# A state-space stage with the jobs of five engines in another order over its 32 scan steps

## The reference

```python
x = x + mamba(layernorm(x), ...)       # the stage that is changed
x = x + moe_ffn(layernorm(x), ...)     # 8 experts, top 2, capacity 80
x = x + attention(layernorm(x), ...)
x = x + moe_ffn(layernorm(x), ...)

# mamba, d_inner = 512, d_state = 16
xc, z = split(x @ in_proj_w + in_proj_b)
xc = silu(depthwise_conv(xc, 4 taps) + conv_b)
delta_s, B, u = split(xc @ x_proj_w + x_proj_b)
delta = softplus(delta_s @ dt_proj_w + dt_proj_b)
h[t] = exp(-n * delta[t]) * h[t-1] + delta[t] * B[t] * u[t]   # n = 1..16
y[t] = sum over the 16 states of h[t]
out = ((y + u * D) * silu(z)) @ out_proj_w + out_proj_b
```

## Time and profile before

| | us |
|---|---|
| three runs | 3225.42, 3229.64, 3231.66 (median 3229.64) |
| the profiled execution | 3236.31, span 3234.5 |
| first and last scan start | 75.9 and 1659.7 |
| busy over the span: PE, PE weight loads | 2880.0, 2285.2 |
| busy over the span: DVE, ACT, POOL | 2343.9, 1760.0, 2186.3 |
| POOL's products dbu, 512 of them | 1198.1 |
| DVE's scans, 512 of them | 1145.4 |
| ACT's decays da, 1024 of them | 571.3 |

### The profile page before, as it was taken

How to read it: one execution, slowest core, us unless ns; L and a number is a source line. 1 busy time by engine, 2 the same in 40 slices (tenths; PEclk the granted TensorE clock), 3 DMA queues, 4 the chain that set the end, 5 groups by cost and what they waited for, 6 DMA issues and landing times. The chain is left out here.

```text
span 3234.5 us, 54379 instructions
## 1 busy us (share of the span) xinstructions
PE 2880.0 (89%) x16992; PEld 2285.2 (71%) x16992; DVE 2343.9 (72%) x4219; ACT 1760.0 (54%) x3332; POOL 2186.3 (68%) x1405
## 2 busy tenths in 40 slices
PE   5899989999899898999857999996999985999998
PEld 2566666666666665666547999996777775999998
DVE  2998889888898888988965666564566654666564
ACT  3766767667676566766534444452333333444443
POOL 2888988889888898899955555552233435565554
PEclk8999999999999999999978999997999997999999
DMA  4231222112221122211244445442222223444443
GB/s 106 104 112 67 81 74 71 45 55 81 75 73 42 55 81 76 72 44 53 74 159 137 115 105 129 94 116 53 76 85 85 89 80 111 116 111 110 105 116 48
DMA packets 192660, 281.60 MB, mean 87 GB/s; under 512 B 35943, under 2 KB 164622, under 8 KB 184264
## 3 DMA queue, kind: packets, MB, share of 16 engines
q1 hardware_dynamic: 157128, 236.31, 22.1%
q0 software_dynamic: 35328, 42.76, 7.4%
HBM read 197.28 MB, written 94.72 MB: 90 GB/s over the span
## 5 line engine op out<-in xcount | busy, mean ns | idle before, releaser
L605 POOL TENSOR_TENSOR dbu<-du,bb 128x1024 f32<-128x1024 f32 x512 | 1198.1, 2362 | 66.2 <-DVE hs L755 63.0
L755 DVE TENSOR_TENSOR_SCAN hs<-da,dbu 128x1024 f32<-128x1024 f32 x512 | 1145.4, 2275 | 49.4 <-POOL dbu L605 20.9
L690 ACT ACTIVATE da<-delta 128x512 f32<-128x512 f32 x1024 | 571.3, 595 | 270.2 <-DVE hs L755 249.4
L855 PEld LDWEIGHTS yT<-ident,hs 128*128 128x128 f32 x4096 | 501.7, 150 | 162.3 <-issue 115.1
L855 PE MATMUL yT<-ident,hs 128*128 128x128 f32 x4096 | 552.2, 288 | 27.4 <-DVE hs L755 27.2
L1322 POOL TENSOR_TENSOR ffn_w_lo<-ffn_w,ffn_w_hi 128x512 fp32r<-128x512 f32 x256 | 344.1, 1370 | 177.8 <-ACT ffn_w_hi L1317 173.6
L1368 PE MATMUL ffn_hbank<-ffn_rowsT_hi,ffn_w_hi 128*128 128x320 f32 x1024 | 341.4, 333 | 43.7 <-DVE ffn_hT_lo L1390 41.5
L1402 PE MATMUL ffn_ybank<-ffn_w_hi,ffn_hT_hi 128*128 128x256 f32 x1280 | 365.1, 285 | 0.7 <-DVE ffn_hT_lo L1390 0.7
L1404 PE MATMUL ffn_ybank<-ffn_w_hi,ffn_hT_lo 128*128 128x256 f32 x1280 | 359.5, 281 | 0.0
L1403 PE MATMUL ffn_ybank<-ffn_w_lo,ffn_hT_hi 128*128 128x256 f32 x1280 | 359.3, 281 | 0.0
L1370 PE MATMUL ffn_hbank<-ffn_rowsT_hi,ffn_w_lo 128*128 128x320 f32 x1024 | 322.2, 315 | 0.0
(11 more groups left out here) (237 smaller groups left out, 5271.1 us busy)
## 6 DMA issues: line engine op xcount, KB each, us to landing
bb<-b_rows SPq DMA_DIRECT2D x64, 1024.0 KB, 4.5
ffn_w<-L_ffn_W SPq DMA_DIRECT2D x64, 1024.0 KB, 10.1
slots<-empty SPq DMA_DIRECT2D x40, 530.0 KB, 6.5
ffn_rows<-slots SPq DMA_DIRECT2D x32, 662.5 KB, 5.0
a_x<-x_after_mamba SPq DMA_DIRECT2D x32, 512.0 KB
xt<-L_attn_a_x SPq DMA_DIRECT2D x16, 512.0 KB
x<-L_attn_a_x SPq DMA_DIRECT2D x16, 512.0 KB, 4.1
x_after_mamba<-x SPq DMA_DIRECT2D x16, 512.0 KB, 2.9
```

The source lines that it names most:

```text
L605: pool.tensor_tensor(dbu[:, s % DEEP], du[:, dt, :].unsqueeze(1).to_broadcast([P, SN, T]), bb[:, q * SN:(q + 1) * SN, :], ALU.mult).then_i ...
L690: ins = act.activation(da[:, s % 2, i, :], delta[:, par, dt, :], ACT.Exp, scale=-float(q * SN + i + 1))
L755: dve.tensor_tensor_scan(flat[0], flat[1], flat[2], 0.0, ALU.mult, ALU.add).then_inc(scanned.sem, 1)
L855: mm = pe.matmul(yT[:, j * P:(j + 1) * P], hs[:, s % DEEP, i, j * P:(j + 1) * P], k.ident[:], start=False, stop=(q == QS - 1 and i == SN - ...
```

## The change

The arithmetic and the number of instructions stay. What changes is at which of the 32 steps each engine does its other jobs, the order of jobs within some steps, and with that the four lists of orders, and so the bank of some jobs in the ring and the job whose reader they wait for: O0 goes ahead of T0 and T1, I1 ahead of O1, and RP ahead of Z3. No step's own work (dbu, da, scan, sum) moves.

```diff
-RING_JOBS = ("G3", "Z0", "U2", "T0", "O0", "T1", "U3", "I0", "O1", "I1", "G0", "Z1", "I2", "I3", "S", "RT0", "RT1",
-             "DA0", "DA1", "DA2", "DA3", "G1", "RL", "U0", "Z2", "U1", "G2", "Z3", "RP", "-")
+RING_JOBS = ("G3", "Z0", "U2", "O0", "T0", "T1", "U3", "I0", "I1", "O1", "G0", "Z1", "I2", "I3", "S", "RT0", "RT1",
+             "DA0", "DA1", "DA2", "DA3", "G1", "RL", "U0", "Z2", "U1", "G2", "RP", "Z3", "-")
...
-DVE_JOBS = ("G3", "Z0", "O0", "I0", "O1", "G0", "I1", "Z1", "I2", "I3", "G1", "RL", "Z2", "G2", "RP", "Z3")
+DVE_JOBS = ("G3", "Z0", "O0", "I0", "I1", "O1", "G0", "Z1", "I2", "I3", "G1", "RL", "Z2", "G2", "RP", "Z3")
```

More of the change, by code:

```diff
@@ L1003, in one_turn @@
                             decay_step(act, row, 1 - par, s)
-                        if s == 0 and late:
+                        if s == 1 and late:
                             gate_input(act, turn, 3)
-                        if s == 1 and late:
                             summed_copy(act, turn, turn - 2, 3)
@@ L1033, in one_turn @@
                             tanh_x(act, turn, 2)
-                        if s == 16 and late:
-                            route_apply(act, turn, turn - 2)
                         if s == 17 and first:
                             tanh_x(act, turn, 3)
-                        if s == 18 and main:
-                            summed_copy(act, turn, row, 1)
+                        if s == 17 and late:
+                            route_apply(act, turn, turn - 2)
+                            route_turned(act, turn, 0)
                         if s == 18 and is_turn(turn, 0):
@@ L1042, in one_turn @@
                             act.wait_ge(skip_ready, 1)
+                        if s == 19 and main:
+                            summed_copy(act, turn, row, 1)
                         if s == 19 and first:
@@ L1045, in one_turn @@
                         if s == 19 and late:
-                            route_turned(act, turn, 0)
                             route_turned(act, turn, 1)
-                        if s == 20 and first:
+                        if s == 21 and first:
                             step_size(act, turn, par, 0)
-                        if s == 21 and first:
                             step_size(act, turn, par, 1)
@@ L1127, in one_turn @@
                             route_stats(dve, turn, turn - 2)
-                        if s == 15 and first:
+                        if s == 15 and main:
+                            silu_z(dve, turn, 1)
+                        if s == 16 and first:
                             silu_x(dve, turn, 2)
-                        if s == 16 and first:
                             silu_x(dve, turn, 3)
-                        if s == 22 and main:
+                        if s == 23 and main:
                             gate(dve, turn, 1)
@@ L1167, in one_turn @@
                             pe.wait_ge(staged, STAGED)
-                        if s == 1 and first:
-                            turn_x(pe, turn, 0)
                         if s == 1 and late:
@@ L1173, in one_turn @@
                         if s == 2 and first:
+                            turn_x(pe, turn, 0)
+                        if s == 3 and first:
                             turn_x(pe, turn, 1)
@@ L1198, in one_turn @@
                             conv_taps(pe, turn, 3)
[L1199 to L1201 removed]
                             x_proj_small(pe, turn, 0)
+                        if s == 13 and late:
+                            route_turn(pe, turn, turn - 2, 0)
+                        if s == 14 and late:
+                            route_turn(pe, turn, turn - 2, 1)
                         if s == 15 and first:
                             x_proj_small(pe, turn, 1)
[L1205 to L1207 removed]
                         if s == 16 and first:
```

120 lines of the change are left out of this document (58 added, 62 removed).

## The result

| | before | after |
|---|---|---|
| median of 20 runs each, us | 3228.51 (3221.66 to 3233.14) | 3216.23 (3207.38 to 3225.69) |
| profiled execution, its span, us | 3236.31, 3234.5 | 3207.38, 3205.6 |
| first and last scan start, us | 75.9 and 1659.7 | 70.0 and 1648.1 |

The ratio is 0.9964, with a 95% interval of 0.9955 to 0.9973: the change wins 12.3 us. The profiled execution of after happens to be the fastest of its 20. Its span is 28.9 us shorter, but only 11.5 us of that lie up to the last scan. The rest arises in later stages, whose code did not change, so the stage has to be read by its scans. So two medians can differ by some us that do not come from the stage.

The account below looks back on a forecast made before the run. DVE, POOL and PE were taken as nearly full, leaving only DVE's 9 to 13 us of standing per turn. 5.5 + 1.2 + 8 x 1.1 - 5 x 0.5 - 3.0 = 10.0 us, from 3229.64 to 3219.6; range 3195 to 3241.

Parts of the forecast that it names:

- eight quiet turns: Turns without the hardware loop's jump (3, 4, 6, 8, 10, 12, 14, 15): each wins 1.1 us.
- The ends: First and last turns: 5.5 us won before the first scan, 1.2 in the second turn, the others 0.
- What bounds the kernel: Steady turn: DVE, POOL and PE have under a tenth of slack; only DVE's 9 to 13 us standing can be won.
- Steps 0 to 9: Quiet turn: two DVE waits go, du 3 waits for U3 instead; scan 9 again at 29.2, gain 0.
- Steps 9 to 13: Quiet turn: the 1.70 us wait for the first tanh is covered; statistics end at 47.4 instead of 49.3, gain 1.6 to 1.8.
- Steps 13 to 25: Quiet turn: ACT's run from decay 19 grows from 18.2 to some 20.1 us; about 0.6 given back, scan 25 at 78.2.
- The 3.0 us for scan 31: Steps 25 to 31: behind PE's 3.66 us stop, sum 27 comes too late for scan 31; 0.5 us in 6 turns.
- The loop turn: Turn begun by the loop's jump: ACT's last uD ends 2.1 us later, delaying ysb and PE; loss 0.5 us in five turns.
- Rival 4: Step 13: PE's two new stops (0.7, 0.9 us) bring half clock; 3253.2 us, or 3236.4 if in half the turns; chance 0.18.
- rival 3: Start of each quiet turn: sum 0, G3 and Z0 at half clock, 14.4 us lost in eight turns; 3234.0 us; chance 0.08.

Follow-up runs that it names:

- Run 2: Changed kernel, but in turn 0 alone ScalarE again makes the first tanh ahead of the second convolution's input; first scan at 72.89 us instead of 70.03.
- run 6: Changed kernel with POOL's eight scatters at every second step (1, 3 ... 15) instead of steps 1 to 8; ratio to before 0.9966.
- Run 5: Kernel before with the order of the first tanh alone (and its silu), no job in another bank; ratio to before 0.9984.
- run 9: Run 5 with POOL's two powers for the norms behind its product 16 instead of 17; ratio to before 0.9922, median 3202.78 us.
- 4: Changed kernel with ScalarE's copy of the third block's sums at step 26 instead of 27; ratio to before 0.9946, stage 1575.0 us.
- 8: Changed kernel with the copy of the third block's sums at step 26 and ScalarE's first uD at step 28 instead of 31; ratio to before 0.9944.
- run 3: Changed kernel with VectorE's du of the second block back at step 30 instead of 31; one run of 3220.58 us, stage 1584.0, 5.9 longer.
- 10: Run 6 with POOL's power for the router's norm behind product 15 instead of 16; ratio to before 1.0125.

## Why the prediction was right in sum and wrong in its parts

The forecast was 3219.6 us, 10.0 us off the time before; the stage came 11.5 us earlier and the median fell by 12.3. (The forecast starts from the median of three executions; from that of 20, 3228.51, the same sum gives 3218.5.) The sum is right because its errors cancel, and that is luck. By the table of turns above, in us:

| part | won, forecast | won, measured |
|---|---|---|
| start to first scan | 5.5 | 5.9 |
| second turn (turn 1) | 1.2 | -2.5 |
| eight quiet turns, less the charge for late scans | 8.8 - 3.0 | 3.0 |
| five loop turns | -2.5 | 4.0 |
| turns 2 and 16 | 0 | 1.2 |

- *The ends.* First scan 70.4 forecast, 70.03 measured. Run 2 shows one of the two named causes, the order: 2.9 us in the changed kernel. The other bank takes away its stop, but no run shows it to win anything beside the order. The second turn was to win 1.2 and lost 2.5; scan 6 starts at 23.75 instead of 20.82, and scan 0 of the next turn waits 1.05 us for a decay. No run settles the rest.
- *What bounds the kernel.* "No engine has more than a tenth of slack" passes over ScalarE, which is busy for 68.8 of 98.81 us. But its slack didn't help: the waits for its decays are the largest of after, so what counts there is its order and not its share.
- *Steps 0 to 9: right.* Scan 9 at 29.2, behind POOL; run 6 shows that the sends set it. The du waits 2.4 us for U3 (2.3 forecast), 2.9 in loop turns. What the quiet turns won there in run 6 (2.0 us at scan 9), L175 took back by scan 14.
- *Steps 9 to 13: right in size, wrong in cause.* "Gain about 1.6 to 1.8 us" is what came, if the silu of Z1 (0.58 us), which moved behind, is taken from the 2.4. But I gave it all to the tanh. Run 5 moves the tanh and wins nothing in the quiet turns from 3 to 14; run 9 adds POOL's pause and wins some 2.2 us in each of them. The change has both, so the walk gave the right number. The step said of POOL's power behind dbu 16 that "it costs nothing"; it is what let the gain through. The 0.79 us row of L175 stood in the trace of before and I took it for work.
- *Steps 13 to 25: mis-sized.* "About 0.6 is given back" was 1.3 (1.9 less the silu's 0.58). Decay 19 starts at 58.1, as forecast, but from there to the decays of step 25, at 1040.17, ScalarE's run is 19.5 us long, against 18.2 before, and scans 20, 23 and 25 wait 1.0 us for decays. The step has a slip, too: 58.0 and "some 20.1 us" make 78.1 for the start of those decays, and scan 25 comes 1.2 us behind it (1049.09 and 1050.30 in the earlier trace rows). By its own terms it would be 79.3, no gain at all; its 78.2 asks for a run of 19.0 us. Run 9, with the old order there, gives nothing back: 29.45 us from scan 14 to scan 25, as before (29.44), against 31.3 in the changed kernel. Eight quiet turns at 1.1 became 0.1 to 0.5 each.
- *The 3.0 us for scan 31: right in size, at another scan.* The waits behind PE's stop of 3 us are at scan 28 in six turns and at scan 31 in one of them, 3.1 us together, and they go with the stop in runs 4 and 8. The step gave no reason for its six turns; that there were six is luck.
- *The loop turn: wrong sign.* "Loss 0.5 us" assumed that ScalarE's stop of 4.25 us stays behind a later uD. It fell to 1.9 to 2.1, so decay 0 comes 3.0 to 3.2 us ahead of scan 0, where it had 3.2 to 3.5. And the later du, which I counted as the cause of the loss, keeps PE's long stop further from Z0: run 3, without it, is 5.9 us slower, in its one profile. The loop turns won 4.0 us in all, with a spread of 2.8 us that goes with the clock at which Z0 runs. Why the clock is back before Z0 in two turns of the five isn't shown; the tanh's part in the 4.0 us isn't either, but run 5, with the tanh alone, won 5.5 there.
- *The rivals.* Rival 4 had no part: PE's two new stops came (0.49 and 0.74 us), but from 1001 to 1018 us, steps 12 to 16 of the same quiet turn with both in it, the granted clock is 1.00.

```profile
1001.00:1018.00 17.00, 15.78 (x58) 7.72 (x56) 16.63 (x31) 11.05 (x20) 14.54 (x8) 1.00 0.00 0
```

  (The window, its length, busy us and instructions of PE, PE's weight loads, DVE, ACT and POOL, and the granted clock.) Z0 of the quiet turns took 1.88 us behind a stretch of transposes, so rival 3 had no part. The rule of the Trainium skill ("TensorE: Matmul & The Clock Gate", Part 4: PE-mode transpose), that transposes don't bring the full clock, had none either; the trace does not agree with it. In turn 7 the granted clock was 0.50 from 666 to 669 us and 1.00 from 669.5 on, and behind its stop PE had run nothing but transposes until then.

The behaviour of L175 is in the Trainium skill ("SBUF — State Buffer", Who interferes with whom): `cast` and `tensor_scalar` can take the port pair that VectorE shares with GpSimd, `tensor_tensor` with two SBUF inputs contends with GpSimd's reads, and the loser blocks for the other's whole instruction. Runs 5, 9 and 10 agree for L175 (0.17 or 2.46 us), L312 (2.37) and L314 (1.25). They don't agree in two points: the 3.57 us of turn 16 are longer than one product (2.32 us), and the 512 scans, which have two inputs in SBUF, took 2.256 to 2.293 us each, most of them beside products. Not every small instruction is held up: in before the statistics (L168, 0.40 to 0.42 us), the reduction L349 (0.17 to 0.18) and the silu and gate, which read the ring (0.66 to 0.69), took as long inside a product as outside.
